# The last four feature groups take turns, pair 1 is normed in the first stage, and GpSimd's bias add is tied to the start of a tile

## The chip, the core and the metric

The kernel runs on one core of one Trainium2 chip. The metric is the device time of one execution in microseconds (us); lower is better. Before the change the median of three runs is 749.44 us (748.73 to 749.64). The core has a matrix engine (TensorE, PE in the profile), a vector engine (VectorE, DVE), an activation engine (ScalarE, ACT) and GpSimd (POOL). Each runs its own list of instructions in order; they meet only at semaphores. SyncE (SP) issues the transfers here.

## The reference

The input x has 4 x 1024 rows (tokens) of D = 1024 features. The features are 8 groups of 128, each with its own small network; then comes a layer norm over all 1024 features, modulated by a condition, a SiLU and one full projection.

```python
xr = x.reshape(B, T, 8, 128)
h  = gelu(einsum('btel,elf->btef', xr, W1) + b1)        # 128 -> 512, per group e
y  = (einsum('btef,efl->btel', h, W2) + b2).reshape(B, T, D)
scale, shift = split(silu(emb) @ emb_W + emb_b)
hn = layernorm(y) * ln_g + ln_b;  hn = hn * (1 + scale) + shift
out = x + silu(hn) @ out_W + out_b
```

## The kernel before, in words

Each matrix product in full precision is three products of rounded parts: high x high, low x high, high x low. So each operand is rounded (a cast to "hi") and its rest is subtracted (to "lo").

**First stage.** The 4096 tokens are four quarters of 1024, and there are N = 32 items: item n is one group g on one quarter t, `ORDER[n]` (here NT = 4). An item has C = 4 steps c, one for each 128 of the 512 hidden features; the steps are numbered m = 4n + c, and (n, c) names one. In step m TensorE does `first(m + 2)` (six matmuls into a ring of two pairs of PSUM banks) and then `second(m)` (six matmuls that accumulate y). In between lie, for each step: ScalarE's GELU (L360), the cast to `g_hi` (by ScalarE for c = 3 and 0, L366, by VectorE for c = 1 and 2, L505), and VectorE's `g_lo` (L507). Per item there is also the split of x^T (`xT_hi` L352 on ScalarE, `xT_lo` L495 on VectorE) and ScalarE's `stage_y` (L373), after which the block of y goes to `y_scratch` in HBM.

**Second stage.** The tokens are 16 pairs p of two tiles of 128. A pair is loaded into one of three buffers `yb`, and needs: a tree of adds over the 8 groups (`mean_sum_first` L532, `mean_sum_rest` L537 and L539), a split of the sum (L543, L545), a **row sum** on TensorE (two matmuls with a matrix that holds 1/1024, L761 and L762) that gives the mean; the subtraction (`centre`, L551); squares on ScalarE (L378); the same tree, split and row sum for the variance (L556 to L568); the square root on ScalarE (`root`, L390, with a table load on either side); reciprocal (L573) and multiplication (`norm`, L578) on VectorE; SiLU with the modulation on ScalarE (L448), rounding (L383) and the rest (`rest_s`, L596). Then TensorE projects both tiles q = 2p and 2p + 1, each with 8 groups x 6 matmuls (`project`, L822; the last tile L834). GpSimd adds the output bias to the tile `res` of x (L341), and VectorE's `finish` adds the projection to it (L670).

**What sets the order.** All orders are written out by hand. In the VectorE, ScalarE and TensorE programs of the first stage, extra pieces stand behind `if (n, c) == ...`: they come after the split of step m + 2 (VectorE), after `gelu(m + 2)` (ScalarE), before `first(m + 2)` (TensorE). In this way pair 0 is normed and rounded inside the first stage (items 24 to 30). In the second stage the row sums of later pairs are put between the groups of a projection: `MEAN_AT[p]` and `VAR_AT[p]` are (i, t, g): iteration i, tile t of it, after group g. Iteration i projects pair i, while VectorE norms pair i + 1 and sums pair i + 2. GpSimd's adds wait only for their `res` tile to land (and, the first, for `normed` 4).

Of the kernel before, what the change touches and what calls it, by code (L numbers as in the profile page):

```python
# [5 lines left out]
P = 128  # L6
# [9 lines left out]
def cond_ffn_program(nc, x, xT, vectors, W1, W2, emb_W, out_W, out_b, out):  # L16
# [16 lines left out]
    LATE = range(G - 3, G)  # L33
    ORDER = [(g, t) for g in range(G - 3) for t in range(NT)] + [(g, t) for t in range(NT) for g in LATE]
# [10 lines left out]
    LOADS = [("W", 0), ("W", 1), ("O", 0), ("W", 2), ("O", 1), ("O", 2), ("W", 3), ("O", 3), ("O", 4), ("W", 4),  # L45
             ("O", 5), ("W", 5), ("O", 6), ("W", 6), ("O", 7), ("W", 7)]
    SPLIT_ITEM = [None, 1, 2, 3, 5, 6, 7, 9, 10, 11, 12, 13, 14, 15, 17, 19]
# [4 lines left out]
    Y0_MEAN_AT = (25, 1)  # L52
    Y0_VAR_AT = (27, 1)
# [3 lines left out]
    LAG = 9  # L57
    MEAN_AT = {1: (0, 0, 0), 2: (0, 1, 6)}
    VAR_AT = {1: (0, 1, 0)}
# [5 lines left out]
    MEAN_OF = {at: p for p, at in MEAN_AT.items()}  # L65
    VAR_OF = {at: p for p, at in VAR_AT.items()}

# [16 lines left out]
    with ExitStack() as ctx:  # L84
# [31 lines left out]
        R0 = S0 + 9728  # L116
# [13 lines left out]
        yb0 = at("yb0", [P, G, TP], R0)  # L130
        s_lo0 = at("s_lo0", [P, G, TP], R0 + 8 * KB, F32R)
        s_hi0 = at("s_hi0", [P, G, TP], R0 + 16 * KB, F32R)
        s_hi1 = at("s_hi1", [P, G, TP], R0 + 24 * KB, F32R)
        s_lo1 = at("s_lo1", [P, G, TP], R0 + 32 * KB, F32R)
        res = at("res", [P, 4, D], R0 + 48 * KB)
        yb1 = at("yb1", [P, G, TP], R0 + 104 * KB)
        sq = at("sq", [P, G, TP], R0 + 112 * KB)
        out_b_all = at("out_b_all", [P, D], R0 + 120 * KB)
        yb2 = at("yb2", [P, G, TP], R0 + 124 * KB)
# [52 lines left out]
        y0_var = sem("y0_var")  # L192
# [34 lines left out]
        var_ps = psum[:, 5, 0:TP]  # L227
        rstd_ps = psum[:, 6, 0:TP]
# [12 lines left out]
        def _(sp):  # L241
# [32 lines left out]
            for n in range(N):  # L274
                if n + 2 < N:
                    sp.wait_ge(xlo_done, n + 1)
                    load_x(n + 2)
                j = 0 if n == 0 else SPLIT_AT.get(n - 1)
                if j == 0:
                    sp.wait_ge(w_split, 2)  # L280
                    load_raw(2)
                if n - 1 in SPLIT_AT and SPLIT_AT[n - 1] + 2 < len(LOADS):
                    sp.wait_ge(w_split, 2 * (SPLIT_AT[n - 1] + 1))
                    load_raw(SPLIT_AT[n - 1] + 2)
                if n - 1 in EMB_ITEM[:-1]:
# [3 lines left out]
                if n == Y0_ITEM + 1:  # L289
                    sp.wait_ge(emb_chunk, KE)  # L290
                    for s in range(2):
                        sp.wait_ge(y_stored[s], 16 * len(range(s, Y0_ITEM + 1, 2)))
                    for p in range(3):
                        load_y(p)
                if n == N - 1:
                    sp.dma_start(out_b_all[:], out_b.rearrange("(o d) -> o d", o=1).to_broadcast([P, D])
                                 ).then_inc(out_b_landed, 16)
# [45 lines left out]
        @block.scalar  # L343
        def _(act):
# [40 lines left out]
            def root(p, var):  # L385
                nc.scalar.preload_act_table(ACT.Sqrt)
                if p == 0:
                    act.wait_ge(y0_var, 1)
                act.wait_ge(var_done, p + 1)
                nc.scalar.activation(std[:], var, ACT.Sqrt, bias=eps[:]).then_inc(std_done, 1)  # L390

            def tanh_y0(h):
                act.wait_ge(y0_halved, (h + 1) * HG)
                nc.scalar.activation(sq[:, half_of(h)], yb0[:, half_of(h)], ACT.Tanh).then_inc(y0_tanh, 1)
# [16 lines left out]
            for m in range(M):  # L411
# [10 lines left out]
                if (n, c) == (25, 3):  # L422
                    square(0, 0)
                if (n, c) == (26, 0):
                    square(0, 1)
                if (n, c) == (29, 3):
# [9 lines left out]

            stage_y(N - 1)
            square(1, 0)
            square(1, 1)
            root(1, var_ps)  # L440
            nc.scalar.preload_act_table(ACT.Silu)
# [17 lines left out]
        def _(dve):  # L459
# [110 lines left out]

            def invert(p, rstd):
# [16 lines left out]
            def silu_y0(h):  # L588
                dve.wait_ge(y0_tanh, h + 1)
                part = yb0[:, half_of(h)]  # L590
                nc.vector.scalar_tensor_tensor(part, sq[:, half_of(h)], 1.0, part, ALU.add, ALU.mult
# [10 lines left out]
            for m in range(M):  # L602
# [21 lines left out]
                if (n, c) == (24, 0):  # L624
                    mean_sum_first(0)
                if (n, c) == (24, 1):
                    mean_sum_rest(0)
                if (n, c) == (24, 2):
                    mean_split_up(0)
                if (n, c) == (25, 1):  # L630
                    centre(0, 0, small(25)[:, 0:TP])
                if (n, c) == (25, 2):
                    centre(0, 1, small(25)[:, 0:TP])
                if (n, c) == (26, 0):
                    var_sum_first(0)
                if (n, c) == (26, 1):
                    var_sum_rest(0)
                if (n, c) == (26, 2):
                    var_split_up(0)
                if (n, c) == (27, 1):  # L640
                    dve.wait_ge(var_done, 1)
                    nc.vector.tensor_copy(total[:], small(27)[:, 0:TP]).then_inc(y0_var, 1)
                if (n, c) == (28, 1):
                    invert(0, total[:])
                if (n, c) == (28, 2):
                    norm(0, 0, total[:])
                if (n, c) == (29, 0):
                    halve_y0(0)
                if (n, c) == (29, 1):
                    norm(0, 1, total[:])  # L650
                if (n, c) == (29, 2):
                    halve_y0(1)
                if (n, c) == (30, 0):
                    silu_y0(0)
                if (n, c) == (30, 1):
                    silu_y0(1)
                if (n, c) == (30, 2):
                    rest_s(0, 0)
                if (n, c) == (30, 3):
                    rest_s(0, 1)  # L660
                if (n, c) == (31, 1):
                    mean_sum_first(1)
                if (n, c) == (31, 2):
                    mean_sum_rest(1)
                    mean_split_up(1)
# [6 lines left out]
            centre(1, 0, mean_ps)  # L672
            centre(1, 1, mean_ps)
            var_sum_first(1)
            var_sum_rest(1)
            var_split_up(1)
# [32 lines left out]
        def _(pe):  # L709
# [53 lines left out]


# [16 lines left out]
            for m in range(M):  # L781
# [7 lines left out]
                if (n, c) == Y0_MEAN_AT:  # L789
# [4 lines left out]
                if (n, c) == Y0_VAR_AT:  # L794
                    pe.wait_ge(y_staged, n)
                    pe.wait_ge(var_split, 2)
                    row_sum(small(n)[:, 0:TP]).then_inc(var_done, 1)
# [7 lines left out]
                if c == 0:  # L805
# [4 lines left out]
                    if n - 1 == Y0_MEAN_AT[0]:  # L810
                        pe.wait_ge(centred, 2)
                    if n - 1 == Y0_VAR_AT[0]:
                        pe.wait_ge(y0_var, 1)
# [24 lines left out]
            def mean_of(p):  # L838
                if p == 1:
                    pe.wait_ge(y_staged, N - 1)  # L840
                pe.wait_ge(mean_split, 2 * p + 2)
                row_sum(mean_ps).then_inc(mean_done, 1)

            def var_of(p):
                pe.wait_ge(var_split, 2 * p + 2)
                row_sum(var_ps).then_inc(var_done, 1)

            for i in range(NP):
                ahead = i + 2
                for t in range(2):  # L850
# [8 lines left out]
                    for g in range(G):  # L859
# [3 lines left out]
                        if (i, t, g) in MEAN_OF:  # L863
                            mean_of(MEAN_OF[i, t, g])
                        if (i, t, g) in VAR_OF:
                            var_of(VAR_OF[i, t, g])
# [32 lines left out]
```

## Time and profile before

| | before |
|---|---|
| median of three runs | 749.44 us |
| the profiled execution | 750.59 us |
| its span on the core | 748.8 us |
| TensorE busy | 727.6 us, 97% |
| VectorE busy | 581.6 us, 78% |
| ScalarE busy | 453.4 us, 61% |
| GpSimd busy | 83.1 us, 11% |
| mean granted TensorE clock | 0.993 |

The span is cut by the profiler from the first to the last instruction; the 1.8 us between it and the execution's time lie around it. The first stage lasts to 368.7 us, the second from there to the end. A TensorE busy share of 97% leaves 21 us in which it was idle; a chain of waits and a list of who waited for whom tell where these lie.

### The profile page before, as it was taken

What the parts mean: (1) busy time and instruction counts of PE and PEld (TensorE: products, weight loads), DVE (VectorE), ACT (ScalarE), POOL (GpSimd) and SP (SyncE); (2) the same over time, 40 slices, a digit from 0 to 9 for tenths busy, and PEclk for the clock granted to TensorE, in tenths of its full rate; (3) what the DMA queues carried; (4) which work ended last, traced back from release to release, by engine and by line L of the source; (5) the groups of instructions that cost most, each with busy time, mean ns of one, the idle gap of its engine ahead of it and who ended that gap; (6) DMA issues with size and microseconds to landing.
All of it is one profiled execution on the core that took longest, in us unless ns stands there. A gap on an engine that the chain in (4) does not pass through costs nothing.

```text
span 748.8 us, 8254 instructions
## 1 busy us (share of the span) xinstructions
PE 727.6 (97%) x3208; PEld 587.3 (78%) x3208; DVE 581.6 (78%) x626; ACT 453.4 (61%) x494; POOL 83.1 (11%) x38
## 2 busy tenths in 40 slices
PE   9999999999999999999987999999999999999998
PEld 6887777877778888888775888888877787777886
DVE  6887878878778768969868888888879787798811
ACT  7777677776777877988651665564446453464500
POOL 0000000000000000000022122222112221132210
PEclk9999999999999999999998999999999999999999
DMA  6435446554453155222613234444422344331321
GB/s 227 127 125 170 144 166 196 183 184 150 160 169 112 57 192 202 74 96 84 205 48 130 91 121 165 141 168 169 169 112 92 133 169 163 119 113 56 113 85 56
DMA packets 42470, 101.77 MB, mean 136 GB/s; under 512 B 3136, under 2 KB 23616, under 8 KB 39360
## 3 DMA queue, kind: packets, MB, share of 16 engines
q1 hardware_dynamic: 41760, 100.73, 38.3%
q8 instruction: 25, 0.41, 0.2%
q10 hardware_dynamic: 672, 0.52, 0.2%
q14 instruction: 13, 0.11, 0.0%
HBM read 67.69 MB, written 33.55 MB: 135 GB/s over the span
## 4 chain that ended last, share of the span: by engine, by line
PE 83%; DVE 14%; ACT 1%; issue 1%; DMA 0%; ACTq 0%
PE psum L822 36%; PE psum L721 22%; PE psum L737 22%; DVE sq L537 3%; DVE yb L578 3%; DVE psum L573 2%; DVE sq L532 2%; PE psum L834 1%; PE psum L747 1%; DVE res L670 1%; DVE sum_lo L545 1%; DVE g_lo L507 1%; DVE total L539 1%; PE psum L761 1%; DVE sum_hi L543 1%
## 5 line engine op out<-in xcount | busy, mean ns | idle before, releaser
L507 DVE TENSOR_TENSOR g_lo<-g_raw,g_hi 128x1024 fp32r<-128x1024 f32 x128 | 156.6, 1225 | 70.7 <-ACT g_hi L366 68.2
L360 ACT ACTIVATE g_raw<-psum,cols 128x1024 f32<-128x1024 f32 x128 | 142.7, 1116 | 61.5 <-PE psum L721 46.5
L822 PE MATMUL psum<-oW_hi,s_hi 128*128 128x512 f32 x496 | 154.3, 392 | 0.0
L822 PE MATMUL psum<-oW_hi,s_lo 128*128 128x512 f32 x496 | 153.9, 392 | 0.0
L822 PE MATMUL psum<-oW_lo,s_hi 128*128 128x512 f32 x496 | 153.9, 391 | 0.0
L341 POOL TENSOR_TENSOR res<-res,out_b_all 128x1024 f32<-128x1024 f32 x32 | 82.4, 2579 | 637.1 <-DVE yb L578 386.1
L737 PE MATMUL psum<-g_hi,W 128*128 128x512 f32 x512 | 137.7, 391 | 0.8 <-DVE g_hi L505 0.5
L721 PE MATMUL psum<-xT_hi,W 128*128 128x512 f32 x508 | 137.2, 392 | 0.1
L721 PEld LDWEIGHTS psum<-xT_hi,W 128*128 128x128 f32 x508 | 94.4, 188 | 26.6 <-issue 7.6
L737 PEld LDWEIGHTS psum<-g_hi,W 128*128 128x128 f32 x512 | 95.7, 188 | 23.0 <-DVE emb_rows L616 1.8
L822 PEld LDWEIGHTS psum<-oW_lo,s_hi 128*128 128x128 f32 x496 | 93.7, 189 | 20.0
L822 PEld LDWEIGHTS psum<-oW_hi,s_lo 128*128 128x128 f32 x496 | 93.7, 189 | 19.8
L822 PEld LDWEIGHTS psum<-oW_hi,s_hi 128*128 128x128 f32 x496 | 92.2, 190 | 17.4
L448 ACT ACTIVATE yb<-yb,mod_c,mod_a 128x256 f32<-128x256 f32 x120 | 62.3, 591 | 29.5 <-DVE yb L578 29.5
L737 PE MATMUL psum<-g_lo,W 128*128 128x512 f32 x256 | 79.1, 390 | 0.1
L721 PE MATMUL psum<-xT_lo,W 128*128 128x512 f32 x254 | 78.3, 389 | 0.0
L670 DVE TENSOR_TENSOR res<-psum,res 128x1024 f32<-128x1024 f32 x31 | 37.9, 1222 | 46.6 <-PE psum L822 46.4
L366 ACT CAST g_hi<-g_raw 128x1024 fp32r<-128x1024 f32 x64 | 67.2, 1051 | 10.2 <-PE psum L737 9.0
L378 ACT ACTIVATE sq<-yb 128x1024 f32<-128x1024 f32 x32 | 34.0, 1063 | 60.8 <-DVE yb L551 59.7
L737 PEld LDWEIGHTS psum<-g_lo,W 128*128 128x128 f32 x256 | 47.8, 188 | 10.8 <-DVE g_lo L507 0.9
L390 ACT ACTIVATE std<-psum,eps 128x256 f32<-128x256 f32 x15 | 7.2, 477 | 80.5 <-PE psum L762 80.5
L721 PEld LDWEIGHTS psum<-xT_lo,W 128*128 128x128 f32 x254 | 47.7, 188 | 10.1
(80 smaller groups left out, 636.5 us busy)
## 6 DMA issues: line engine op xcount, KB each, us to landing
y_scratch<-y_stage SPq DMA_DIRECT2D x32, 512.0 KB, 3.1
yb<-y_scratch SPq DMA_DIRECT2D x16, 1024.0 KB, 4.8
res<-in_x SPq DMA_DIRECT2D x32, 512.0 KB, 5.1
xT_raw<-in_xT SPq DMA_DIRECT2D x31, 512.0 KB, 4.6
out<-res SPq DMA_DIRECT2D x31, 512.0 KB, 2.8
emb_raw<-in_emb_W SPq DMA_DIRECT2D x8, 1024.0 KB, 7.4
wraw<-in_out_W SPq DMA_DIRECT2D x16, 256.0 KB, 5.1
wraw<-in_W SPq DMA_DIRECT2D x14, 256.0 KB, 4.9
```

Of the source, the lines that this page charges most:

```text
L341: nc.gpsimd.tensor_tensor(res[:, q % 4], res[:, q % 4], out_b_all[:], ALU.add).then_inc(res_biased, 1)
L360: nc.scalar.activation(g_raw[:, m % 2], ring(m), ACT.Gelu, bias=cols[:, R_B1 + k:R_B1 + k + 1]).then_inc(gelu_done, 1)
L366: nc.scalar.copy(g_hi[:, m % 2], g_raw[:, m % 2]).then_inc(ghi_act, 1)
L378: nc.scalar.activation(sq[:, half_of(h)], yb[p % 3][:, half_of(h)], ACT.Square).then_inc(squared, 1)
L448: nc.scalar.activation(yb[p % 3][:, g], yb[p % 3][:, g], ACT.Silu, scale=mod_a[:, b, g:g + 1], bias=mod_c[:, b, g:g + 1]).then_inc(silu_do ...
L507: nc.vector.tensor_tensor(g_lo[:, m % 2], g_raw[:, m % 2], g_hi[:, m % 2].bitcast(F32), ALU.subtract).then_inc(glo_done, 1)
L537: nc.vector.tensor_tensor(sq[:, 0:2], sq[:, 0:2], sq[:, 2:4], ALU.add).then_inc(mean_tree, 1)
L578: nc.vector.tensor_tensor(part, part, rstd.unsqueeze(1).to_broadcast([P, HG, TP]), ALU.mult).then_inc(normed, 1)
L670: nc.vector.tensor_tensor(res[:, q % 4], proj(q), res[:, q % 4], ALU.add).then_inc(out_ready, 1)
L721: mm = nc.tensor.matmul(ring(m)[:, half], W[:, g % WS, w, cut], v[:, n % 2, half], start=(k == 0), stop=(k == 2))
L737: mm = nc.tensor.matmul(y_psum(n)[:, half], W[:, g % WS, w, cut], v[:, m % 2, half], start=(c == 0 and k == 0), stop=(c == C - 1 and k == 2))
L822: mm = nc.tensor.matmul(proj(q)[:, half], v[:, g, cut], w[:, g, half], start=(g == 0 and k == 0), stop=(g == G - 1 and k == 2))
```

## The change

1. `LATE` is now the last four groups instead of the last three: the items 16 to 31 go through groups 4, 5, 6, 7 for each quarter in turn. So quarter 0 is complete after item 19 instead of item 22, and pairs 0 and 1 are loaded from `y_scratch` at item 20. The order of the weight loads and of their splits is adapted.
2. Pair 1 is normed in the first stage too: its mean row sum is at step (27, 1), its variance row sum at (30, 1), pair 0's are at (23, 1) and (25, 1) (before: (25, 1) and (27, 1)). Its root, reciprocal and multiplication remain at the start of the second stage.
3. In the second stage every pair from 2 on has its mean row sum after group 7 of the first tile and its variance row sum after group 7 of the second: `(p - 2, 0, 7)` and `(p - 2, 1, 7)`.
4. GpSimd's add of tile q waits for `proj_done` q, that is for the end of tile q - 1; the add of tile 0 waits for the reciprocal of pair 1.
5. `yb2`, `s_hi0` and others lie elsewhere; the load of pair 2 is moved from item 23 to item 31, behind the load of pair 3 and a wait for the last `first`. The bias row `out_b` is loaded at item 20. The variance and reciprocal rows use PSUM banks 7 and 5, and pair 0's reciprocal has a buffer `rstd0` of its own.

```diff
-    LATE = range(G - 3, G)
+    LATE = range(HG, G)
...
-    for p in range(2, NP):
-        late = max(LAG - p, 0)
-        VAR_AT[p] = (p - 1, 0, late - 1) if late else (p - 2, 1, 7)
-        if p > 2:
-            MEAN_AT[p] = (p - 2, 1, late) if late else (p - 2, 0, 6)
+    MEAN_ITEM = {23: 0, 27: 1}
+    VAR_ITEM = {25: 0, 30: 1}
+    MEAN_OF = {(p - 2, 0, 7): p for p in range(2, NP)}
+    VAR_OF = {(p - 2, 1, 7): p for p in range(2, NP)}
...
                     sp.wait_ge(emb_chunk, KE)
...
-                    for p in range(3):
+                    for p in range(2):
                         load_y(p)
                 if n == N - 1:
...
                     sp.wait_ge(slo_done, 2)
                     load_y(3)
-                    sp.wait_ge(xlo_done, N)
+                    sp.wait_ge(s1_done, M)
+                    load_y(2)
                     for q in range(2):
                         load_res(q)
...
             pool.wait_ge(out_b_landed, 16)
-            pool.wait_ge(normed, 4)
             for q in range(QN):
+                if q == 0:
+                    pool.wait_ge(rstd_done, 2)
+                else:
+                    pool.wait_ge(proj_done, q)
                 pool.wait_ge(res_landed[q % 4], 16 * (q // 4 + 1))
...
-                if (n, c) == (28, 0):
+                if (n, c) == (26, 0):
                     root(0, total[:])
                     nc.scalar.preload_act_table(ACT.Gelu)
...
+            root(1, total[:])
+            nc.scalar.preload_act_table(ACT.Silu)
             stage_y(N - 1)
...
+                if (n, c) == (26, 1):
+                    invert(0, rstd0[:])
+                if (n, c) == (26, 2):
+                    norm(0, 0, rstd0[:])
+                if (n, c) == (26, 3):
+                    mean_sum_rest(1)
+                    mean_split_up(1)
+                if (n, c) == (27, 0):
+                    halve_y0(0)
                 if (n, c) == (27, 1):
+                    centre(1, 0, small(27)[:, 0:TP])
+                if (n, c) == (27, 2):
+                    centre(1, 1, small(27)[:, 0:TP])
...
+                if c == 1 and n in MEAN_ITEM:
                     pe.wait_ge(y_staged, n)
                     pe.wait_ge(ones_ready, 1)
-                    pe.wait_ge(mean_split, 2)
-                    row_sum(small(n)[:, 0:TP]).then_inc(mean_done, 1)
+                    mean_of(MEAN_ITEM[n], small(n)[:, 0:TP])
```

The first place is VectorE's program in the first stage, where the reciprocal and the first multiplication of pair 0 stand (`yb_77` is the buffer of pair 0). Before, item 28 and the start of item 29:

```order
L507 TENSOR_TENSOR g_lo<-g_raw,g_hi 128x1024 x2
L573 RECIPROCAL total<-std 128x256
L507 TENSOR_TENSOR g_lo<-g_raw,g_hi 128x1024
L578 TENSOR_TENSOR yb_77<-yb_77,total 128x1024
L495 TENSOR_TENSOR xT_lo<-xT_raw,xT_hi 128x1024
L505 CAST g_hi<-g_raw 128x1024
L507 TENSOR_TENSOR g_lo<-g_raw,g_hi 128x1024
L505 CAST g_hi<-g_raw 128x1024
```

After, item 26 and the start of item 27, where the last `g_lo` is that of step (27, 1), `yb_78` is pair 0's buffer and `rstd_67` its reciprocal:

```order
L512 TENSOR_TENSOR g_lo<-g_raw,g_hi 128x1024 x2
L582 RECIPROCAL rstd_67<-std 128x256
L512 TENSOR_TENSOR g_lo<-g_raw,g_hi 128x1024
L587 TENSOR_TENSOR yb_78<-yb_78,rstd_67 128x1024
L500 TENSOR_TENSOR xT_lo<-xT_raw,xT_hi 128x1024
L510 CAST g_hi<-g_raw 128x1024
L512 TENSOR_TENSOR g_lo<-g_raw,g_hi 128x1024
L542 TENSOR_TENSOR sq<-sq 128x512
L544 TENSOR_TENSOR total<-sq 128x256
L548 CAST sum_hi<-total 128x256
L550 TENSOR_TENSOR sum_lo<-total,sum_hi 128x256
```

The seven rows up to that `g_lo` are the same; behind them now stand the four instructions that make pair 1's mean sum, on which the row sum at (27, 1) waits. The second place is GpSimd's program in the second stage, with the semaphores each add waits for. Before, its second, third and fourth add:

```order
L341 TENSOR_TENSOR res<-res,out_b_all 128x1024 [waits res_landed1]
L341 TENSOR_TENSOR res<-res,out_b_all 128x1024 [waits res_landed2]
L341 TENSOR_TENSOR res<-res,out_b_all 128x1024 [waits res_landed3]
```

After:

```order
L342 TENSOR_TENSOR res<-res,out_b_all 128x1024 [waits res_landed1,proj_done]
L342 TENSOR_TENSOR res<-res,out_b_all 128x1024 [waits res_landed2,proj_done]
L342 TENSOR_TENSOR res<-res,out_b_all 128x1024 [waits res_landed3,proj_done]
```

Every add now waits for the end of the tile before its own as well.

## Rows read from the trace of the kernel before

**Rows 1.** Waits of PE over the whole span: us in total, times, longest us

```profile
PE psum L761 <- DVE sum_lo L545: 15.1, 9, 7.8
```

**Rows 2.** Timeline of PE: start us, us, line, work, [idle before <- releaser]

```profile
398.68 0.58 PE L761 MATMUL psum<-sum_hi,ones_r 128*128 128x256 f32 x1 [7.81 <-DVE sum_lo L545]
...
399.27 1.05 PE L822 MATMUL psum<-oW_hi,s_hi 128*128 128x512 f32 x2
...
402.41 0.62 PE L822 MATMUL psum<-oW_lo,s_hi 128*128 128x512 f32 x2
...
547.36 0.38 PE L761 MATMUL psum<-sum_hi,ones_r 128*128 128x256 f32 x1 [1.76 <-DVE sum_lo L545]
...
548.63 0.86 PE L822 MATMUL psum<-oW_hi,s_lo 128*128 128x512 f32 x2
...
552.50 0.63 PE L822 MATMUL psum<-oW_lo,s_hi 128*128 128x512 f32 x2
```

**Rows 3.** Windows: us, busy us of PE, PEld, DVE, ACT, POOL, PEclk, DMA

```profile
549.00:552.00 3.00, 3.00 (x9) 2.32 (x8) 2.48 (x3) 0.09 (x1) 0.00 (x0) 0.50 0.14 57
```

**Rows 4.** The chain that ended last (item 26, then two iterations): start us, us, what

```profile
305.45 1.66 PE psum L737 x6
...
411.89 10.90 PE psum L822 x48
...
432.81 10.91 PE psum L822 x48
...
572.84 12.27 PE psum L822 x54
...
596.16 12.26 PE psum L822 x54
```

**Rows 5.** Timeline of DVE, POOL and PE in a late iteration

```profile
585.12 1.23 DVE L670 TENSOR_TENSOR res<-psum,res 128x1024 f32<-128x1024 f32 x1 [3.07 <-PE psum L822]
...
590.65 3.15 POOL L341 TENSOR_TENSOR res<-res,out_b_all 128x1024 f32<-128x1024 f32 x1 [3.30 <-DMA res<-in_x]
...
591.57 2.78 DVE L537 TENSOR_TENSOR sq<-sq 128x512 f32<-128x512 f32 x1
...
595.17 0.43 DVE L545 TENSOR_TENSOR sum_lo<-total,sum_hi 128x256 fp32r<-128x256 f32 x1
...
595.65 0.38 PE L761 MATMUL psum<-sum_hi,ones_r 128*128 128x256 f32 x1 [0.79 <-DVE sum_lo L545]
```

**Rows 6.** Timeline of POOL and DVE: an add beside the reciprocal

```profile
537.46 2.40 POOL L341 TENSOR_TENSOR res<-res,out_b_all 128x1024 f32<-128x1024 f32 x1 [14.85 <-DMA res<-in_x]
...
537.96 1.76 DVE L573 RECIPROCAL psum<-std 128x256 f32<-128x256 f32 x1 [0.88 <-ACT std L390]
```

**Rows 7.** Timeline of DVE: from the mean to the end of the variance sum

```profile
423.07 2.35 DVE L551 TENSOR_TENSOR yb<-yb,psum 128x1024 f32<-128x1024 f32 x2 [1.10 <-PE psum L762]
...
429.33 0.43 DVE L568 TENSOR_TENSOR sum_lo<-total,sum_hi 128x256 fp32r<-128x256 f32 x1
```

**Rows 8.** Timeline of PE and DVE, items 28 and 29, and a mean sum

```profile
340.23 1.07 PE L721 MATMUL psum<-xT_hi,W 128*128 128x512 f32 x4
...
341.11 1.23 DVE L507 TENSOR_TENSOR g_lo<-g_raw,g_hi 128x1024 fp32r<-128x1024 f32 x1
...
342.25 0.69 DVE L505 CAST g_hi<-g_raw 128x1024 fp32r<-128x1024 f32 x1
...
368.98 0.69 DVE L537 TENSOR_TENSOR sq<-sq 128x512 f32<-128x512 f32 x1
...
370.49 0.43 DVE L545 TENSOR_TENSOR sum_lo<-total,sum_hi 128x256 fp32r<-128x256 f32 x1
```

**Rows 9.** Timeline of PE: the first projection of the second stage

```profile
368.71 0.62 PE L822 MATMUL psum<-oW_hi,s_hi 128*128 128x512 f32 x2
```

**Rows 10.** DMA issues from 235 to 300 us: median us to landing last

```profile
yb<-y_scratch SPq DMA_DIRECT2D x3, 1024.0 KB, 7.7
```

**Rows 11.** Windows, columns as in rows 3, then DMA share and GB/s

```profile
369.30:371.30 2.00, 1.17 (x7) 0.70 (x6) 1.52 (x4) 0.72 (x1) 0.00 (x0) 1.00 0.97 401
```

More of the change, by code:

```diff
@@ L29, in cond_ffn_program @@
     assert L == P and D == G * L and T == TA and D == 2 * BANK and C == 4 and G == 8 and NT == 4
-    LATE = range(G - 3, G)
-    ORDER = [(g, t) for g in range(G - 3) for t in range(NT)] + [(g, t) for t in range(NT) for g in LATE]
+    LATE = range(HG, G)
+    ORDER = [(g, t) for g in range(HG) for t in range(NT)] + [(g, t) for t in range(NT) for g in LATE]
     N = len(ORDER)
@@ L41, in cond_ffn_program @@
     WS = 4
-    LOADS = [("W", 0), ("W", 1), ("O", 0), ("W", 2), ("O", 1), ("O", 2), ("W", 3), ("O", 3), ("O", 4), ("W", 4),
-             ("O", 5), ("W", 5), ("O", 6), ("W", 6), ("O", 7), ("W", 7)]
-    SPLIT_ITEM = [None, 1, 2, 3, 5, 6, 7, 9, 10, 11, 12, 13, 14, 15, 17, 19]
+    LOADS = [("W", 0), ("W", 1), ("O", 0), ("W", 2), ("O", 1), ("O", 2), ("W", 3), ("O", 3), ("W", 4), ("O", 4),
+             ("W", 5), ("O", 5), ("W", 6), ("O", 6), ("W", 7), ("O", 7)]
+    SPLIT_ITEM = [None, 1, 2, 3, 5, 6, 7, 8, 9, 10, 11, 12, 13, 14, 16, 19]
     LOAD_OF = {u: j for j, u in enumerate(LOADS)}
@@ L115, in cond_ffn_program @@
         total = at("total", [P, TP], S0 + 8704)
-        R0 = S0 + 9728
+        rstd0 = at("rstd0", [P, TP], S0 + 9728)
+        R0 = S0 + 10752
         emb_raw = at("emb_raw", [P, 2 * D], R0)
@@ L130, in cond_ffn_program @@
         yb0 = at("yb0", [P, G, TP], R0)
+        tanh0 = at("tanh0", [P, G, TP], R0 + 8 * KB)
         s_lo0 = at("s_lo0", [P, G, TP], R0 + 8 * KB, F32R)
-        s_hi0 = at("s_hi0", [P, G, TP], R0 + 16 * KB, F32R)
-        s_hi1 = at("s_hi1", [P, G, TP], R0 + 24 * KB, F32R)
-        s_lo1 = at("s_lo1", [P, G, TP], R0 + 32 * KB, F32R)
+        s_hi1 = at("s_hi1", [P, G, TP], R0 + 16 * KB, F32R)
+        s_lo1 = at("s_lo1", [P, G, TP], R0 + 24 * KB, F32R)
         res = at("res", [P, 4, D], R0 + 48 * KB)
+        yb2 = at("yb2", [P, G, TP], R0 + 64 * KB)
         yb1 = at("yb1", [P, G, TP], R0 + 104 * KB)
@@ L191, in cond_ffn_program @@
         var_done = sem("var_done")
-        y0_var = sem("y0_var")
+        var_copied = sem("var_copied")
         std_done = sem("std_done")
@@ L226, in cond_ffn_program @@
         mean_ps = psum[:, 4, 0:TP]
-        var_ps = psum[:, 5, 0:TP]
-        rstd_ps = psum[:, 6, 0:TP]
+        rstd_ps = psum[:, 5, 0:TP]
+        var_ps = psum[:, 7, 0:TP]
         def half_of(h):
@@ L289, in _ @@
                 if n == Y0_ITEM + 1:
+                    sp.dma_start(out_b_all[:], out_b.rearrange("(o d) -> o d", o=1).to_broadcast([P, D])
+                                 ).then_inc(out_b_landed, 16)
                     sp.wait_ge(emb_chunk, KE)
@@ L386, in root @@
                 nc.scalar.preload_act_table(ACT.Sqrt)
-                if p == 0:
-                    act.wait_ge(y0_var, 1)
+                if p < 2:
+                    act.wait_ge(var_copied, p + 1)
                 act.wait_ge(var_done, p + 1)
+                if p >= 1:
+                    act.wait_ge(rstd_done, p)
                 nc.scalar.activation(std[:], var, ACT.Sqrt, bias=eps[:]).then_inc(std_done, 1)
@@ L421, in _ @@
                     gelu(m + 2)
-                if (n, c) == (25, 3):
+                if (n, c) == (23, 3):
                     square(0, 0)
-                if (n, c) == (26, 0):
+                if (n, c) == (24, 0):
                     square(0, 1)
-                if (n, c) == (29, 3):
+                if (n, c) == (27, 3):
+                    square(1, 0)
+                if (n, c) == (28, 0):
+                    square(1, 1)
+                if (n, c) == (29, 0):
                     tanh_y0(0)
@@ L569, in var_split_up, with copy_var @@
                                         ).then_inc(var_split, 1)
+            def copy_var(p, var):
+                dve.wait_ge(var_done, p + 1)
+                nc.vector.tensor_copy(total[:], var).then_inc(var_copied, 1)
             def invert(p, rstd):
@@ L590, in silu_y0 @@
                 part = yb0[:, half_of(h)]
-                nc.vector.scalar_tensor_tensor(part, sq[:, half_of(h)], 1.0, part, ALU.add, ALU.mult
+                nc.vector.scalar_tensor_tensor(part, tanh0[:, half_of(h)], 1.0, part, ALU.add, ALU.mult
                                                ).then_inc(y0_silu, 1)
@@ L623, in _ @@
                     modulation()
-                if (n, c) == (24, 0):
+                if (n, c) == (21, 1):
                     mean_sum_first(0)
+                if (n, c) == (21, 2):
+                    mean_sum_rest(0)
+                if (n, c) == (22, 0):
+                    mean_split_up(0)
+                if (n, c) == (23, 1):
+                    centre(0, 0, small(23)[:, 0:TP])
+                if (n, c) == (23, 2):
+                    centre(0, 1, small(23)[:, 0:TP])
                 if (n, c) == (24, 1):
-                    mean_sum_rest(0)
+                    var_sum_first(0)
@@ L628, in _ @@
                 if (n, c) == (24, 2):
-                    mean_split_up(0)
+                    var_sum_rest(0)
+                    var_split_up(0)
+                if (n, c) == (25, 0):
+                    mean_sum_first(1)
                 if (n, c) == (25, 1):
[L631 to L635, printed above, removed]
+                    copy_var(0, small(25)[:, 0:TP])
@@ L643, in _ @@
+                if (n, c) == (27, 0):
+                    halve_y0(0)
+                if (n, c) == (27, 1):
+                    centre(1, 0, small(27)[:, 0:TP])
+                if (n, c) == (27, 2):
+                    centre(1, 1, small(27)[:, 0:TP])
+                if (n, c) == (28, 0):
+                    norm(0, 1, rstd0[:])
                 if (n, c) == (28, 1):
-                    invert(0, total[:])
+                    var_sum_first(1)
                 if (n, c) == (28, 2):
-                    norm(0, 0, total[:])
+                    var_sum_rest(1)
@@ L647, in _ @@
                 if (n, c) == (29, 0):
-                    halve_y0(0)
+                    var_split_up(1)
                 if (n, c) == (29, 1):
-                    norm(0, 1, total[:])
+                    halve_y0(1)
                 if (n, c) == (29, 2):
-                    halve_y0(1)
-                if (n, c) == (30, 0):
                     silu_y0(0)
                 if (n, c) == (30, 1):
+                    copy_var(1, small(30)[:, 0:TP])
                     silu_y0(1)
@@ L658, in _ @@
                     rest_s(0, 0)
-                if (n, c) == (30, 3):
+                if (n, c) == (31, 0):
                     rest_s(0, 1)
[L661 to L665, printed above, removed]
             def finish(q):
@@ L670, in finish @@
                 nc.vector.tensor_tensor(res[:, q % 4], proj(q), res[:, q % 4], ALU.add).then_inc(out_ready, 1)
[L672 to L676, printed above, removed]
             for i in range(NP):
@@ L762, in row_sum, with mean_of, var_of @@
                 return nc.tensor.matmul(ps, ones_r[:], sum_lo[:], start=False, stop=True)
+            def mean_of(p, ps):
+                pe.wait_ge(mean_split, 2 * p + 2)
+                row_sum(ps).then_inc(mean_done, 1)
+            def var_of(p, ps):
+                pe.wait_ge(var_split, 2 * p + 2)
+                row_sum(ps).then_inc(var_done, 1)
             pe.wait_ge(emb_copied, 1)
@@ L788, in _ @@
                     turn(n)
-                if (n, c) == Y0_MEAN_AT:
+                if c == 1 and n in MEAN_ITEM:
                     pe.wait_ge(y_staged, n)
                     pe.wait_ge(ones_ready, 1)
-                    pe.wait_ge(mean_split, 2)
-                    row_sum(small(n)[:, 0:TP]).then_inc(mean_done, 1)
-                if (n, c) == Y0_VAR_AT:
+                    mean_of(MEAN_ITEM[n], small(n)[:, 0:TP])
+                if c == 1 and n in VAR_ITEM:
                     pe.wait_ge(y_staged, n)
-                    pe.wait_ge(var_split, 2)
-                    row_sum(small(n)[:, 0:TP]).then_inc(var_done, 1)
+                    var_of(VAR_ITEM[n], small(n)[:, 0:TP])
                 if m + 2 < M:
@@ L809, in _ @@
                         pe.wait_ge(emb_copied, KE + 2)
[L810 to L813, printed above, removed]
+                    if n - 1 in MEAN_ITEM:
+                        pe.wait_ge(centred, 2 * MEAN_ITEM[n - 1] + 2)
+                    if n - 1 in VAR_ITEM:
+                        pe.wait_ge(var_copied, VAR_ITEM[n - 1] + 1)
                 second(m)
@@ L836, in project_halves @@
                     mm.then_inc(proj_done, 1)
[L838 to L846, printed above, removed]
             for i in range(NP):
-                ahead = i + 2
                 for t in range(2):
@@ L863, in _ @@
                         if (i, t, g) in MEAN_OF:
-                            mean_of(MEAN_OF[i, t, g])
+                            if i == 0:
+                                pe.wait_ge(y_staged, N)
+                            mean_of(MEAN_OF[i, t, g], mean_ps)
                         if (i, t, g) in VAR_OF:
-                            var_of(VAR_OF[i, t, g])
+                            var_of(VAR_OF[i, t, g], var_ps)
 def kernel(**inputs):
```

21 lines of the change are left out of this document (2 added, 19 removed).

## The prediction

> **What bounds the kernel now.** I read the page first: TensorE is busy for 727.6 of 748.8 us, so only its idle time and its slow time can be won. Next the list of waits of TensorE: one pair holds nearly all of its idle time, the row sum L761 that waits for VectorE's `sum_lo` L545, 15.1 us in 9 waits [rows 1]. All nine are of the mean's sum in the second stage (its line is L545; the variance's is L568). Then the timeline of PE: the longest wait, 7.81 us, is where pair 2's mean is due while pair 1 is still being normed, another is 1.76 us [rows 2]; the other seven have 5.5 us together, 0.79 each: one, pair 1's, at the start of the stage and six in the late iterations, of which [rows 5] shows one. [...] From 548.63 to 552.50 five pairs of matmuls take 3.87 us, where five pairs at full speed take 5 x 0.455 = 2.27: 1.6 us lost, 1.7 with the edges. Behind the 7.81 us wait four pairs take 3.14 us for 1.82, and the row sum 0.59 for 0.23: 1.7 again [rows 2]. No such stretch follows a 0.79 us wait.
>
> Last the chain, for the cost of a short wait beyond its idle time. An early iteration without a wait goes from 411.89 to 432.81, 20.92 us for 90 matmuls and both row sums; with the other six matmuls (1.36) it would be 22.28. A late one goes from 572.84 to 596.16, 23.32 [rows 4]. The difference is 1.04 for an idle time of 0.79: each wait costs 0.25 beyond what the list says.
>
> So the second stage's loss is 15.1 + 9 x 0.25 + 2 x 1.7 = 20.8 us. All of it hangs on one chain of work on VectorE.
>
> **The change, part by part.**
>
> *Second stage, mean row sums one group later and GpSimd's adds at the start of a tile.* In the late iteration VectorE begins with `finish` at 585.12 and ends `sum_lo` at 595.60: 10.48 us. Of this, L537 takes 2.78 us, because GpSimd's add runs from 590.65 to 593.80 [rows 5]; the same instruction alone takes 0.69 [rows 8]. So the chain is 10.48 - 2.09 = 8.4 us. With the add at the tile's start it would run from about 0.1 to 2.5 or 3.2 us, beside `finish`, the reciprocal and `norm`. That these suffer no delay is seen at 537.96: the reciprocal starts 0.5 us into an add and takes 1.76 us [rows 6]. [...]
> The mean's row sum now stands after 48 matmuls, 10.90 us [rows 4], instead of 42 (9.5): 8.4 against 10.9 leaves 2.5 us. The variance: from the mean's row sum, VectorE needs 423.07 to 429.76, 6.7 us [rows 7]; ahead of it `finish` of the same tile's end takes 1.2. 7.9 against 10.9 leaves 3.0. That the mean now comes after group 7 instead of 6 costs the variance nothing, because `centre` stood behind `finish`, which waits for group 7 anyway. So the eight waits from pair 2 on go, with both slow stretches: bound below, all; bound above, an add that is 3.15 us long and blocks to its end, 8.4 + 3.15 = 11.55, would leave 0.65 + 0.25 per iteration.
>
> *Pair 1 normed in the first stage.* Its mean chain and wait at the start of the second stage (0.79 + 0.25) go. Its root, reciprocal and `norm` (about 0.5 + 1.8 + 2.4) stay ahead of pair 2's mean, which is due 10.9 us into the stage; `centre`, squares and variance tree are no longer there, and this is what takes the 7.81 us away. The four row-sum matmuls move from stage to stage, at nothing net. What comes late next is on TensorE in the first stage.
>
> *The row sum at (27, 1).* VectorE's item 26 is now, instruction by instruction, what item 28 was, root, reciprocal and `norm` included; so its times can be read off, with everything taken relative to the same step. There `g_lo` of step (29, 1) is issued at 341.11 and the next instruction starts at 342.25 [rows 8]. In the new program this next instruction is the first of the four that make pair 1's mean sum (`mean_sum_rest`, `mean_split_up`). They take from 368.98 to 370.92 elsewhere, 1.94 us [rows 8], so `sum_lo` would be there at 344.2, and the row sum starts 0.05 us behind it, as it does at 595.65 [rows 5]. TensorE is at that step at 340.23 [rows 8]: 4.0 us lost, 4.1 with the ramp. Before, three steps lay between a split of the sum and its row sum; here only two do, and `g_lo` of the very step at which TensorE waits is ahead of the sum in VectorE's queue. Behind the waiting row sum on TensorE stand `first` of (27, 3) and `second` of (27, 1), so nothing else can fill the time; VectorE and ScalarE use it to catch up, and I see no later wait in items 27 to 31. 4.1 us lies between 1.76 and 7.81, both of which were followed by a slow stretch that cost 1.7: I take 1.7, bounds 0 and 3.4.
>
> *The other hand-overs.* Pair 0's mean now has five steps, its variance three as before, pair 1's variance five. Each mean in the first stage delays one `second` that waits for `centre` (1.66 instead of 1.36 [rows 4]); there is one more: +0.3. VectorE's extra work is some 9 us for pair 1 (trees and splits 2 x 3.2, `centre` 2.3, copy 0.4) over items 25 to 30; an item's own work there is four `g_lo` and one `xT_lo` at 1.14 (341.11 to 342.25) and two casts at 0.7 [rows 8], 7.1 us; its 48 matmuls take 10.9, which leaves 3.8, and only item 26 gets more (reciprocal 1.76, `norm` 1.14, mean sum 1.94: 4.8), which the wait above pays for. The 0.5 us wait for `g_hi` at the stage's end may go, since one `rest_s` moves behind a split; but `g_lo` of the last step ends when it did, so I count nothing. The tables of weight loads change by one item here and there; TensorE waited for none of them, and I count nothing, bound +1.
>
> *The loads at the turn of the stages.* The load of pair 2 now comes at item 31, behind pair 3's. The stage begins at 368.71 [rows 9]; by an estimate both are issued some 1.8 us ahead of that, behind the `rest_s` that moved, at 366.9, and pair 2's lands as in the burst of three loads, 7.7 us later [rows 10], at 374.6; with 3.2 us for the mean tree and split that is 377.8, due at 368.71 + 10.9 = 379.6. The first residual tile then lands at some 376, at the 401 GB/s of the window [rows 11], and its add ends by 379. It fits with 0.6 to 1.8 us to spare: nothing in the sum, and a rival.
>
> **The sum.** -20.8 + 4.1 + 1.7 + 0.3 = -14.7 us. The profiled execution: span 748.8 to 734.1, its time 750.6 to 735.9. That execution is 1.15 us above the median of 749.44, so against the median I predict 734.7.
>
> **Rivals.**
> 1. *No wait at (27, 1).* If VectorE's backlog behind the root is smaller than in item 28, or the split is there early. For: what VectorE does ahead of item 26 is not all the same as what it did ahead of item 28, so its lead may differ. Against: the chain itself is read off an identical list. Time: 734.7 - 5.8 = 728.9.
> 2. *The turn of the stages waits.* Pair 2 or the first residual lands 2 to 4 us late, because the y stores share the queue; `mean_sum_first` of pair 2 or `finish` of tile 0 then holds all that VectorE has behind it, and a row sum waits about 2 us: 2 + 0.25 + 1.7 = 4. For: the spare time is under 2 us. Time: 738.7.
> 3. *The adds still collide*, the change doing on GpSimd not what it is for: 14 iterations x 0.9 = 12.6, 747.3. For: an add can start late if its tile lands late. Against: a tile lands more than a tile ahead of its use in every late iteration.
> 4. *Slower than before: VectorE's load in the first stage is not hidden.* Place: items 25 to 30, where pair 1's 9.0 us of VectorE and 2.1 us of squares on ScalarE are added. If none of it found room and each of its four pieces (mean tree, `centre`, variance tree, squares) were followed by a slow stretch of 1.7, that would be 11.1 + 6.8 = 17.9, 752.6. It decides once the first stage loses over 20.8 us in all. Against: the 3.8 us free per item.
>
> **Chances.** Forecast 0.64, rival 1 0.12, rival 2 0.15, rival 3 0.04, rival 4 0.02, something unseen 0.03. Its own range is 731.5 to 737.5 (the clock 0 to 3.4, the loads +1). Taking in rivals 1 and 2 gives 728.5 to 740. Faster by over 0.2% (1.5 us, what a measurement can tell from no change): 0.97; within: 0.01; slower: 0.02.
>
> **What would show it.** In the profile after: TensorE's list of waits has one of about 4 us for the mean's `sum_lo`, near 318 us, and none above 0.3 us in the second stage. The slow clock appears once, behind it. An iteration takes 22.3 us throughout. L537's and L532's longest is near their median. GpSimd's adds start within 0.2 us of a tile's start. It is wrong if iterations still take 23.3, if the wait near 318 us is absent or over 6, or if a wait at some 380 us has taken its place.

## The result, and the profile after

The changed kernel takes 735.80 us (median of 4 runs, 735.27 to 736.68) against 749.54 (748.73 to 749.78): a ratio of 0.982, 95% interval 0.9803 to 0.9837. Predicted were 734.7, within 731.5 and 737.5. On a second chip it took 736.64 against 748.54, a ratio of 0.9833 (0.9818 to 0.9848). The profiled execution took 736.68 us with a span of 734.9; before it was 750.59 and 748.8.

I read the same views in the same order. First the longest of the waits of PE over the whole span (us in total, times, longest), where [rows 1] had 15.1 us in 9:

```profile
PE psum L774 <- DVE sum_lo L550: 3.9, 1, 3.9
```

The second stage has none left. There is one in the first stage, at step (27, 1). The timeline of PE shows it, and the slow matmuls behind it; six of the same shape took 1.36 us before and take 2.56 here:

```profile
317.79 1.07 PE L750 MATMUL psum<-g_hi,W 128*128 128x512 f32 x4
...
323.24 0.55 PE L774 MATMUL psum<-sum_hi,ones_r 128*128 128x256 f32 x1 [3.93 <-DVE sum_lo L550]
323.59 0.41 PE L775 MATMUL psum<-sum_lo,ones_r 128*128 128x256 f32 x1
323.80 1.91 PE L734 MATMUL psum<-xT_hi,W 128*128 128x512 f32 x4
...
326.36 1.91 PE L750 MATMUL psum<-g_hi,W 128*128 128x512 f32 x4
...
328.92 1.20 PE L734 MATMUL psum<-xT_hi,W 128*128 128x512 f32 x4
```

On VectorE, the timeline of the same stretch is what [rows 8] gave for item 28, with the sum's four instructions behind the last `g_lo`:

```profile
313.99 1.75 DVE L582 RECIPROCAL rstd<-std 128x256 f32<-128x256 f32 x1
...
320.02 1.23 DVE L512 TENSOR_TENSOR g_lo<-g_raw,g_hi 128x1024 fp32r<-128x1024 f32 x1
321.16 0.69 DVE L542 TENSOR_TENSOR sq<-sq 128x512 f32<-128x512 f32 x1
...
322.67 0.43 DVE L550 TENSOR_TENSOR sum_lo<-total,sum_hi 128x256 fp32r<-128x256 f32 x1
```

The granted clock, in the windows of the same stretch (columns as in [rows 3]), is 0.50 behind the wait and back at 1.00 after 330:

```profile
324.00:328.00 4.00, 4.00 (x11) 3.10 (x10) 2.25 (x5) 1.11 (x1) 0.00 (x0) 0.50 0.00 0
330.00:334.00 4.00, 4.00 (x19) 3.33 (x18) 3.01 (x3) 3.94 (x5) 0.00 (x0) 1.00 0.00 0
```

In the second stage the chain that ended last is nothing but TensorE, 48 matmuls and a row sum in turn. From 565.60 to 587.88, two tiles, is 22.28 us, where [rows 4] had 23.32 in a late iteration:

```profile
565.60 10.91 PE psum L841 x48
576.50 0.12 PE psum L774
...
587.88 10.91 PE psum L841 x48
```

Of VectorE's instructions that read only SBUF, two are still held by an add: the cast L548 of pair 2 (2.38 us, below) and one L605 (`s_lo`) out of 32, at 700.22, with 2.40 us in place of 1.22. TensorE waited for neither. All 16 L542 (L537 before, of which [rows 5] shows one with 2.78 us) take 0.69 us on average, as their row among the groups of VectorE's lines says (busy us, mean ns):

```profile
L542 DVE TENSOR_TENSOR sq<-sq 128x512 f32<-128x512 f32 x16 | 11.1, 691 | 0.5
```

GpSimd's first add starts when its tile of x has landed, 6.9 us into tile 0, and lasts 2.60 us. The other 31 begin within 0.2 us of a tile's start and last 2.41 us each (before 2.4 to 3.25), as its timeline shows:

```profile
409.49 2.41 POOL L342 TENSOR_TENSOR res<-res,out_b_all 128x1024 f32<-128x1024 f32 x1 [8.73 <-PE psum L841]
420.63 2.41 POOL L342 TENSOR_TENSOR res<-res,out_b_all 128x1024 f32<-128x1024 f32 x1 [8.73 <-PE psum L841]
```

By stages, each measured from the start of the first projection matmul in PE's timeline: the second begins at 376.07 instead of 368.71, 7.4 us later, and lasts 358.8 instead of 380.1, 21.3 us less. Together 13.9 us of span.

### The profile page after: what moved, and what is told of

It reads as the page before. It is cut to its first block, busy times and chain, and to the rows that moved or that the text cites. A ratio compares the mean times of both kernels' runs of the same rounds, so it can differ in the third digit from the quotient of the medians.

```text
span 734.9 us, 8303 instructions
## 1 busy us (share of the span) xinstructions
PE 725.1 (99%) x3208; PEld 587.3 (80%) x3208; DVE 551.6 (75%) x627; ACT 453.3 (62%) x494; POOL 78.0 (11%) x38
## 4 chain that ended last, share of the span: by engine, by line
PE 94%; ACT 2%; DVE 2%; issue 1%; DMA 1%; ACTq 0%
PE psum L841 46%; PE psum L734 22%; PE psum L750 22%; PE psum L853 1%; PE psum L760 1%; DVE g_lo L512 1%; ACT g_hi L367 1%; ACT g_raw L361 1%; PE psum L774 1%; DMA wraw<-in_W 1%; PE psum L775 1%; DVE xT_lo L500 0%; ACT xT_hi L353 0%; PE psum L797 0%; ACT L387 0%
## 5 line engine op out<-in xcount | busy, mean ns | idle before, releaser
L342 POOL TENSOR_TENSOR res<-res,out_b_all 128x1024 f32<-128x1024 f32 x32 | 77.3, 2415 | 644.6 <-DMA res<-in_x 381.5
```

## Experiments: what made the long wait

The prediction gave pair 1's norming in the second stage as the cause of the 7.81 us wait (theory A). Read again, the trace of before has another cause in it (theory B). Here is its timeline of VectorE and GpSimd at that wait:

```profile
387.52 10.83 POOL L341 TENSOR_TENSOR res<-res,out_b_all 128x1024 f32<-128x1024 f32 x4 [386.05 <-DVE yb L578]
```

```profile
388.54 2.77 DVE L537 TENSOR_TENSOR sq<-sq 128x512 f32<-128x512 f32 x1
391.35 2.46 DVE L539 TENSOR_TENSOR total<-sq 128x256 f32<-128x256 f32 x1
393.84 2.31 DVE L543 CAST sum_hi<-total 128x256 fp32r<-128x256 f32 x1
396.18 2.44 DVE L545 TENSOR_TENSOR sum_lo<-total,sum_hi 128x256 fp32r<-128x256 f32 x1
```

Four adds run back to back, and each of the four instructions of the mean sum takes about as long as one add: 10.1 us for work that takes 1.94. That is 8.1 us too long, and TensorE waited 7.8. Pair 1's `norm` was done at 387.4, and with the 3.2 us that the mean tree and split take alone `sum_lo` would have been there at about 390.5, in time for TensorE at 390.87. Theory B: the adds made the wait; where pair 1 is normed is second to it. The first four runs, all on one chip, tell them apart.

**The change once more**, as the measure for the others.

> The changed kernel once more, to stand beside the others on the same chip. Both theories: 735.8 us, within 0.5. [...]

Measured: 736.64 us, 735.80 to 736.67. Four of five executions had a mean clock of 0.995, one 0.997; in the four runs on the first chip it was once 0.995 (736.68 us) and three times 0.997 or 0.998 (735.27 to 735.87). The median is 0.84 us over the 735.8 expected, which was to hold within 0.5: here the executions with 0.995 are in the majority. I read the two kinds as a longer and a shorter slow stretch, an estimate from the mean clocks and times alone; they differ by some 0.9 us. Both kept traces are of the kind with 0.995, so the shorter stretch itself was not seen.

**Only GpSimd's edit, on the kernel before.**

```diff
-            pool.wait_ge(normed, 4)
             for q in range(QN):
+                if q == 0:
+                    pool.wait_ge(rstd_done, 2)
+                else:
+                    pool.wait_ge(proj_done, q)
```

> The kernel before with one edit: GpSimd's add of tile q waits for the end of tile q - 1, the first for the reciprocal of pair 1. Pair 1 is still normed in the second stage, pair 2's mean sum still stands where it did. Theory A (as in the prediction: the 7.8 us wait comes from pair 1's norming in the second stage): this wait stays about as long; only the 1.76 and the six 0.79 us waits go, 749.5 - 2.0 - 1.7 - 6.2 = 739.6 us. Theory B (the 7.8 us wait is made by four GpSimd adds in a row that hold VectorE's instructions with two SBUF inputs): here two adds follow each other in place of four, the wait shrinks to about 1.4 us, and the kernel takes 749.5 - 18 = 731.5 us, up to 733.2 if a slow stretch of the clock follows: faster than the whole change.

Measured: 735.80 us (734.90 to 736.77), ratio 0.9825 (0.9808 to 0.9842). The waits of PE, with one row sum's wait of 0.87 us in the total that is pair 1's:

```profile
PE psum L764 <- DVE sum_lo L548: 2.8, 2, 1.9
```

The 7.81 us wait is down to 1.89 with pair 1 where it was. Theory A's "this wait stays" is refuted, B's cause, the adds, is confirmed; its time was too low by 2.6 us and more. Of that 1.1 us is its base: it took the losses of one profiled execution of 750.59 us off a median of 749.5. The wait that is left is 0.5 us longer than its 1.4, and the list has three more waits that B didn't count: two of a row sum of the variance, 0.5 us together, and one of a projection, 0.4. What is left of the wait for the mean has B's cause too. GpSimd's first two adds still follow each other, and the instruction that meets the second takes 2.79 instead of 0.69 (timelines of GpSimd and VectorE):

```profile
385.05 5.76 POOL L344 TENSOR_TENSOR res<-res,out_b_all 128x1024 f32<-128x1024 f32 x2 [383.58 <-DVE psum L576]
```

```profile
388.58 2.79 DVE L540 TENSOR_TENSOR sq<-sq 128x512 f32<-128x512 f32 x1
```

So one edit in one engine's program gives as much as the whole change.

**The same, with the first two adds out of the way and pair 1's mean sum one group later.**

```diff
-            pool.wait_ge(normed, 4)
             for q in range(QN):
+                pool.wait_ge(proj_done, max(q, 1))
...
-    MEAN_AT = {1: (0, 0, 0), 2: (0, 1, 6)}
+    MEAN_AT = {1: (0, 0, 1), 2: (0, 1, 6)}
```

> The kernel before with GpSimd's adds tied to the tiles, the first two both to the end of tile 0 (when VectorE waits for the variance of pair 1), and pair 1's mean row sum one group later. Pair 1 stays in the second stage, the orders of items and row sums are otherwise those of before. Theory B: no row sum in the second stage waits for more than 0.2 us, the clock has no slow stretch, 749.5 - 20.8 = 728.7 us, faster than the changed kernel by 7. Theory A: pair 2's mean sum is still late by several us: 735 to 740 us.

Measured: 731.65 us (731.47 to 731.90), ratio 0.977 (0.9755 to 0.9784). In its second stage no row sum of a mean waits at all; the waits there are of 0.3 us or less, 0.8 together. It is 5 us faster than the changed kernel with pair 1 in the second stage, and its mean clock is 1.0. Theory B again, though 2.9 us over the number expected. The same base explains 1.1 of it, and the three short waits another 1.5, if each costs 0.25 us beyond its idle time as in the prediction.

**The changed kernel without its wait at (27, 1).** Pair 1's tree is finished at (25, 2) and its sum split at (26, 0), ahead of the reciprocal. Pair 0's variance is copied to `rstd0`, so that `total` is free.

```diff
-                nc.vector.tensor_copy(total[:], var).then_inc(var_copied, 1)
+                nc.vector.tensor_copy(total[:] if p else rstd0[:], var).then_inc(var_copied, 1)
...
-                    root(0, total[:])
+                    root(0, rstd0[:])
...
-                if (n, c) == (26, 3):
-                    mean_sum_rest(1)
-                    mean_split_up(1)
+                if (n, c) == (25, 2):
+                    mean_sum_rest(1)
+                if (n, c) == (26, 0):
+                    mean_split_up(1)
```

> The changed kernel, with pair 1's mean tree finished at steps (25, 2) and (26, 0) of VectorE in place of (26, 3); the variance copy of pair 0 goes into rstd0, so that the sum's buffer is free. If the 3.9 us wait at (27, 1) and the slow stretch behind it cost what the trace shows, they go: 735.8 - 4.1 - 1.7 = 730.0 us, down to 729 where the stretch was the long one. Rival: VectorE is so full in items 25 to 27 that the wait only turns up at another step of item 26 or 27: 733 to 736 us.

Measured: 730.18 us (730.16 to 730.32), ratio 0.975 (0.9736 to 0.9765). The timeline of VectorE and that of PE: the sum is there 5.8 us ahead of its row sum, which no longer waits.

```profile
312.98 0.43 DVE L550 TENSOR_TENSOR sum_lo<-total,sum_hi 128x256 fp32r<-128x256 f32 x1
```

```profile
319.18 0.28 PE L775 MATMUL psum<-sum_hi,ones_r 128*128 128x256 f32 x1
```

The wait and its slow stretch cost the changed kernel 6.5 us, and VectorE had the room: the rival fell. The 729 for a longer stretch was an estimate: no execution came below 730.16. This is the fastest version of the study, but only 1.5 us ahead of `tied_no_pair1`, which leaves pair 1 in the second stage.

## Experiments: two covers for one loss

With the wait at (27, 1) gone, the second stage can be tested alone. Two things shield a pair's mean sum from the adds: the adds lie elsewhere, or the row sum comes one group (1.36 us) later. Theory B': either is enough. Of the four runs below, all on one chip, the last three and `early_sum` are the four combinations. "Free" means that an add waits only for its tile to land:

```diff
+            pool.wait_ge(rstd_done, 2)
             for q in range(QN):
-                if q == 0:
-                    pool.wait_ge(rstd_done, 2)
-                else:
-                    pool.wait_ge(proj_done, q)
```

and "group 6" is

```diff
-    MEAN_OF = {(p - 2, 0, 7): p for p in range(2, NP)}
+    MEAN_OF = {(p - 2, 0, 6): p for p in range(2, NP)}
```

**The changed kernel, adds free.**

> The changed kernel without GpSimd's edit: each add waits only for its tile of x to land (the first for the reciprocal of pair 1). Theory B': the mean's chain would be held by 2.1 us, to 10.5 us, but its row sum stands after 10.9 us of matmuls, so nothing waits and the time stays at 736.6 us; the two parts of the change are then two covers for one loss. Rival: the hold reaches the full 3.1 us of an add, or hits the variance chain as well, and the row sums wait 0.6 us and more each, 14 times: 745 to 749 us.

Measured: 739.03 us (736.94 to 740.97), ratio 0.9865 (0.9839 to 0.9891). Of the 14 mean sums 13 come without a wait, as B' had it. One waits 3.33 us: pair 2's, behind four adds in a row that begin when the first tile of x has landed, 5 us after the reciprocal of pair 1 (timelines of GpSimd and PE).

```profile
381.51 9.80 POOL L339 TENSOR_TENSOR res<-res,out_b_all 128x1024 f32<-128x1024 f32 x4 [380.05 <-DMA res<-in_x]
```

```profile
389.20 0.35 PE L771 MATMUL psum<-sum_hi,ones_r 128*128 128x256 f32 x1 [3.33 <-DVE sum_lo L547]
```

I had forgotten this place when I wrote "nothing waits", and the time is 2.4 us over the 736.6 expected. It has the cause of the long wait of before. Pair 1's `centre`, squares and variance tree are in the first stage here, so to have them out of the way is not enough by itself. (The two lengths, 3.33 and 7.81 us, can't be set against each other: pair 2's row sum is due 10.9 us into the stage here and 22.2 us into it before.)

**early_sum, adds free, group 7.**

> The kernel early_sum with the same edit, adds free, mean row sums after group 7. B': 730.2 us as early_sum. Rival: 739 to 743 us.

Measured: 732.09 us (731.41 to 732.21), ratio 0.9771 (0.9754 to 0.9788). L539, the counterpart of L537 in the second stage, is held at nearly every pair, as its row among the groups of VectorE's lines from 376 to 700 us shows (busy us, mean ns; alone it is 690):

```profile
L539 DVE TENSOR_TENSOR sq<-sq 128x512 f32<-128x512 f32 x14 | 34.7, 2480 | 0.5
```

And yet PE waits only once, for pair 2's sum behind the four adds at the start; this accounts for 1.5 of the 1.9 us by which the run lies above `early_sum` and the 730.2 expected:

```profile
PE psum L772 <- DVE sum_lo L547: 1.2, 1, 1.2
```

**early_sum, adds tied, group 6.**

> The kernel early_sum, adds tied as there, but the mean row sums of pairs 2 to 15 after group 6 in place of 7. The chain of 8.4 us fits before 9.5 us: B' expects 730.2 us. Rival (the later row sum is what counts, not the adds): waits of 0.8 us, 14 x 1.04 = 14.6, 744.8 us.

Measured: 731.12 us (730.83 to 731.28), ratio 0.9759 (0.9743 to 0.9776). There is one wait of 0.6 us, pair 2's, and in the profiled executions the second stage is 0.7 us longer than that of early_sum. That is most of the 0.9 us between the medians, and the two chips differ by 0.3 on the kernel before. The rival's 14 waits don't exist.

**early_sum, adds free, group 6.**

> The kernel early_sum with both taken back: adds free and the mean row sums after group 6. Both covers gone, each chain of 8.4 + 2.1 = 10.5 us meets 9.5 us: waits of 0.8 us costing 1.04 each, 14 times: 730.2 + 14.6 = 744.8 us by B'. By the rival that adds don't meet the chain once pair 1 is out of the way: 730 to 732 us.

Measured: 749.13 us (745.06 to 751.72, 10 runs), ratio 1.0001 (0.998 to 1.0022). The whole gain is gone, as the waits of PE show:

```profile
PE psum L772 <- DVE sum_lo L547: 13.0, 14, 2.7
```

| second stage on early_sum | row sum after group 7 | after group 6 |
|---|---|---|
| adds tied to tiles | 730.18 us | 731.12 us |
| adds free | 732.09 us | 749.13 us |

(The first cell is of the other chip; the kernel before took 748.54 there and 748.80 here.) Taking either cover away costs 1 to 2 us, taking both costs 19. B' expected 14.6, and the expected time of 744.8 lies below all ten executions. The profiled one, 748.97 us with a mean clock of 1.0, shows where 4 us of this lie. Its second stage is 16.6 us longer than that of early_sum, which is the 13.0 us of waits and 0.26 beyond for each: 2.0 more than expected, nearly all because pair 2's wait, behind four adds in a row, is 2.69 us and not 0.8. Its first stage, the same program as in early_sum, is 2.1 us longer (371.56 against 369.50), and 1.6 of this is there by the first L748 matmul (12.16 against 10.54). That part is of this execution, not of the edit. The mean clock is 1.0 in four of the ten (745.06 to 748.97) and 0.995 to 0.998 in six (748.45 to 751.72), so a slow stretch behind some of the waits is probably part of the rest in those six; no trace of one was kept.

## Why the prediction was right, and where it was not

**Size and sign** came from the right terms. Against its own profile the change brought 13.9 us of span for 14.7 predicted.

*The gain of the second stage*: 20.8 predicted, 21.3 measured by the stages' lengths. The difference is that two row sums, 0.5 us, moved to the first stage, which I had netted. All iterations with row sums take 22.28 us, the number that was worked out from an early iteration of before. [rows 5]'s blocked instruction is back to 0.69.

*The wait at (27, 1)*: 4.0 us lost predicted from item 28's timeline, 3.93 us of idle time measured, from 319.3 to 323.24, where I had put it near 318. This was the step that the diff did not show and the order did: the sum stands behind a `g_lo` of the very step at which TensorE waits.

*The slow stretch behind it*: the term of 1.7 us was mis-sized. I took 1.7 us, within 0 and 3.4. In the profiled execution the row sum and the two groups of six matmuls behind it take 323.24 to 329.12, 5.9 us in place of 2.95: 2.9 us lost. In executions with a clock of 0.998 it is probably less; between the two kinds lie some 0.9 us. The 1.2 us more than assumed cover the 0.8 us by which the profiled span, 734.9, lies above the 734.1 of the sum; the forecast against the median was low by 1.1, and which part of that is the clock was not measured. The remaining term, 0.3 us for the second `centre`, is borne out by early_sum, which has neither wait nor stretch: its second stage begins at 369.50, 0.8 us later than before, which is 0.3 and the two row sums.

*The cause of the 7.81 us wait*: the step that failed is "`centre`, squares and variance tree are no longer there, and this is what takes the 7.81 us away". With GpSimd's edit alone 5.9 of the 7.8 us go, and with the first two adds moved as well all of it goes, pair 1's norming still in the second stage (only its mean row sum is one group later). With pair 1's part moved and the adds free, 3.33 us of wait are there. That this term came out right is luck: the change also ties the adds, which is what removes the wait. I had also called every mean row sum "one group later". That holds for the late iterations alone; pair 2's is due 11.3 us earlier in the stage than before (10.9 against 22.2), so the wait went although TensorE asks sooner. I had the four instructions at 2.3 to 2.8 us in the timeline of before and used the mechanism for the six short waits, but did not ask the same of the longest one.

*The parts are not a sum.* The prediction gave the gain to the chain and let the later row sum and the tied adds share it. They are substitutes in the steady iterations (last table). And norming pair 1 in the first stage, as it is placed, costs what it brings: GpSimd's edit alone, 735.80 us (734.90 to 736.77), stands beside the whole change at 736.64 (735.80 to 736.67) on that chip. Placed better (early_sum) the whole is worth 18.4 us, of which `tied_no_pair1` gets 16.9 with the adds moved and one row sum one group later.

*The turn of the stages* (rival 2) came close. In the changed kernel the cast L548 of pair 2's sum met the first add and took 2.38 us instead of 0.29; `sum_lo` was ready at 386.2, and TensorE at 387.0:

```profile
382.99 2.60 POOL L342 TENSOR_TENSOR res<-res,out_b_all 128x1024 f32<-128x1024 f32 x1 [381.53 <-DMA res<-in_x]
```

```profile
383.36 2.38 DVE L548 CAST sum_hi<-total 128x256 fp32r<-128x256 f32 x1
```

The landing of pair 2's load had been put 5.9 us into the stage; VectorE could start on it after 4.8. Rival 1 (no wait at (27, 1)) and rival 3 (the adds still collide) are refuted by the waits and by GpSimd's timeline, rival 4 by the first stage's loss of 7.4 us, under the 20.8 at which it would have decided.

## What to carry to other kernels

When a chain is late, look at the duration of each instruction in it before explaining its length by the work it holds: four instructions at 2.3 to 2.8 us that take 0.3 to 0.7 elsewhere were a collision here, and moving the other engine's work (here to the start of a tile, when VectorE reads PSUM) was one edit. Then check that a part of a change isn't paid for by another part: here each cover alone was nearly enough. And when work is put between the steps of a pipeline, count from the instruction that the waiting engine needs back through the queue of the one that makes it; a sum that stands behind the very step's own split comes too late.

## What the runs showed of the hardware

In the changed kernel a cast, with one input in SBUF, was held by GpSimd's add as L537, with two, was in that of before (2.78 us beside an add, 0.69 alone): the 128x256 cast took 2.38 us beside an add and 0.29 alone, while the reciprocal ([rows 6]) and `finish`, with PSUM on one side, kept their 1.76 and 1.22 us. At the long wait of before, with work queued on both engines, four adds took 10.83 us and four instructions of VectorE beside them 10.1, at 2.31 to 2.77 each; I read this as an alternation one for one, an estimate from these durations. A TensorE wait of 1.89 us was followed by no slow stretch in the profiled execution of adds_tied_only (mean clock 1.0), a wait of 1.76 us in that of before was; so the length of the wait alone does not tell whether it costs 1.7 us more. The clock row doesn't show all slow matmuls: in the profiled execution of early_free_g6 the four from 8.59 to 10.29 take 0.43 us each, where four of the same shape from 10.78 to 11.71 take 0.23, and the windows of both say 1.00.
